# A two-stage attention kernel: energies and group mean placed later, row maxima first on VectorE, and the rounding of the two normalised images traded between ScalarE, VectorE and GpSimd

## The reference, cut to what matters

```python
# x: (8, 32, 32, 256), float32: 8 images of 1024 tokens with 256 channels
def stage0(x):    # local attention: 32 windows of 32 tokens, 8 heads of 32
    q, k, v = split(einsum('bnwc,cd->bnwd', x, w_qkv))
    attn = softmax(einsum('bhnqd,bhnkd->bhnqk', q, k) * 32 ** -0.5)
    out = einsum('bhnqk,bhnkd->bhnqd', attn, v)
    return einsum('bnwc,cd->bnwd', out, w_proj) + b_proj
def stage1(x):    # global attention: one head over all 1024 tokens
    q, k, v = x @ Wq, x @ Wk, x @ Wv        # 32, 32 and 256 channels
    energy = einsum('bid,bjd->bij', k, q)
    return gamma * einsum('bij,bjc->bic', softmax(energy), v)
x = x + stage0(group_norm(x))   # 32 groups of 8 channels, over the whole image
x = x + stage1(group_norm(x))
```

## Time and profile before

| | |
|---|---|
| time, median of 3 runs | 740.21 us (739.8 to 742.75) |
| the profiled execution's own time | 739.61 us |
| its span, first to last instruction | 737.8 us, mean granted clock 0.938 |
| PE busy | 601.7 us (82%) |
| DVE busy | 517.4 us (70%) |
| ACT busy | 298.4 us (40%) |
| POOL busy | 193.5 us (26%) |

### The profile page before, as it was taken

One profiled execution on the slowest core, in us unless ns is written; L12 is line 12 of the kernel. 1 busy time (PEld: TensorE's weight loads), 2 busy tenths in 40 slices (PEclk: granted clock), 3 DMA queues, 4 the chain that ended last, 5 costly groups with the idle time before them and its releaser, 6 DMA issues.

```text
span 737.8 us, 14831 instructions
## 1 busy us (share of the span) xinstructions
PE 601.7 (82%) x5859; PEld 433.7 (59%) x5859; DVE 517.4 (70%) x829; ACT 298.4 (40%) x390; POOL 193.5 (26%) x162
## 2 busy tenths in 40 slices
PE   2565694599798988899898988899888989667987
PEld 2255372457575666657674767666665757444756
DVE  4745367777858878687868877786868785854664
ACT  2323242276125741385225631485226631541071
POOL 4512152303304241305203241305212241002000
PEclk9695896899999999999999999999999999978999
DMA  4032315031421224031502323031502212201001
GB/s 149 15 101 58 85 31 136 2 85 31 122 59 40 67 54 136 16 101 30 145 32 57 71 73 90 14 100 28 151 30 70 61 44 80 69 3 36 29 16 58
DMA packets 40306, 47.51 MB, mean 64 GB/s; under 512 B 6848, under 2 KB 32320, under 8 KB 40256
## 3 DMA queue, kind: packets, MB, share of 16 engines
q1 hardware_dynamic: 36960, 43.47, 22.3%
q10 hardware_dynamic: 3296, 3.34, 1.4%
HBM read 10.09 MB, written 8.39 MB: 25 GB/s over the span
## 4 chain that ended last, share of the span: by engine, by line
PE 54%; DVE 22%; issue 8%; ACT 6%; POOL 5%; SPq 3%; DMA 2%; DVEq 0%; ACTq 0%; POOLq 0%
PE pb L250 7%; PE pb L251 6%; PE pb L252 6%; PE pa L250 6%; PE pa L251 6%; PE pa L252 6%; PE pa L484 4%; PE pb L554 3%; POOL b_nl L1042 3%; DVE a_nh L833 3%; PE pb L536 3%; DVE ast L800 3%; SPq L318 2%; DVE max_neg L896 2%; DVE a_rsum L855 2%
## 5 line engine op out<-in xcount | busy, mean ns | idle before, releaser
L250 PE MATMUL pb<-v_h,e_h 128*128 128x257 f16 x464 | 127.4, 275 | 0.0
L252 PE MATMUL pb<-v_h,e_l 128*128 128x257 f16 x464 | 126.4, 272 | 0.0
L251 PE MATMUL pb<-v_l,e_h 128*128 128x257 f16 x464 | 126.0, 272 | 0.0
L896 DVE TENSOR_REDUCE max_neg<-pb 128x1 f32<-128x1024 f32 x64 | 77.3, 1207 | 65.3 <-PE pb L536 65.3
L911 DVE TENSOR_TENSOR e_l<-e,e_h 128x1024 f16<-128x1024 f32 x64 | 77.8, 1223 | 17.1 <-ACT e L738 15.5
L738 ACT ACTIVATE e<-pb,f_energy 128x1024 f32<-128x1024 f32 x64 | 71.3, 1114 | 14.8 <-PE pb L554 14.8
L1049 POOL TENSOR_TENSOR xb<-xin,bias 128x2048 f32<-128x2048 f32 x8 | 36.3, 4537 | 126.6 <-DVE x L876 126.6
L536 PE MATMUL pb<-q_stack,k_stack 96*128 96x512 f16 x128 | 40.4, 399 | 30.7 <-DMA k_stack<-qk_hl 16.3
L686 ACT ACTIVATE a_xT<-a_xT,anb,ar 128x512 f32<-128x512 f32 x32 | 23.4, 802 | 96.9 <-POOL anb L1033 96.9
L250 PE MATMUL pa<-a_nh,wqkv_h 128*128 128x512 f16 x128 | 50.5, 394 | 11.6 <-DVE before_turn L867 6.0
L1054 POOL TENSOR_TENSOR before_turn<-before_turn,a_rinv 128x1024 f32<-128x1024 f32 x16 | 30.6, 1913 | 89.9 <-DVE a_rinv L857 89.9
(11 more groups left out here) (135 smaller groups left out, 1395.6 us busy)
## 6 DMA issues: line engine op xcount, KB each, us to landing
xin<-in_x SPq DMA_DIRECT2D x16, 512.0 KB, 4.6
diag<-qkT SPq DMA_DIRECT2D x64, 128.0 KB, 2.3
diag<-turned SPq DMA_DIRECT2D x64, 128.0 KB, 2.4
turned<-before_turn SPq DMA_DIRECT2D x128, 64.0 KB, 2.0
out<-y SPq DMA_DIRECT2D x24, 256.0 KB, 2.1
out<-y ACTq DMA_DIRECT2D x8, 256.0 KB, 2.1
q_stack<-qk_hl SPq DMA_DIRECT2D x8, 128.0 KB, 2.3
k_stack<-qk_hl SPq DMA_DIRECT2D x8, 128.0 KB, 2.4
```

The lines of the kernel that those rows point to most:

```text
L250: nc.tensor.matmul(out_ap, lh, rh, start=start, stop=False)
L251: nc.tensor.matmul(out_ap, lh, rl, start=False, stop=False)
L252: return nc.tensor.matmul(out_ap, ll, rh, start=False, stop=stop)
L896: nc.vector.tensor_reduce(max_neg[:, it:it + 1], pb[:, 0:2, :].rearrange("p a n -> p (a n)"), X, ALU.max, negate=True).then_inc(b_max, 1)
```

## The change

Nothing is computed differently. The PE list puts energy 0 and energy 1 each half an output block later, and the group mean and variance of the local image one output block later. The DVE list starts the first half with `a_maximum` and moves row sums and transposes behind row maxima; the group steps of the local image move one maximum later. The rounding of the local image (`a_nh`) goes from DVE to ACT, which computes it straight from the copy with a second activation per piece; `a_out_high` goes ahead of it. The low part of the global image (`b_nl`) goes from POOL to DVE, right behind each rounding.

```diff
@@ PE: group_mean, group_var (the same with u["var"])
-                nc.tensor.matmul(pb[:, 2, u["col"]:u["col"] + CT], group_avg[:], u["mv"][:, :, 0], start=True, stop=True).then_inc(u["s_gm"], 1)
+                nc.tensor.matmul(pb[:, u["mean"], u["col"]:u["col"] + CT], group_avg[:], u["mv"][:, :, 0], start=True, stop=True).then_inc(u["s_gm"], 1)
@@ bufs: a gets mean=3, var=2; b gets mean=2, var=3
@@ PE: first
                     if o and not last_image(i - 1): b_output(i - 1, it, b, range(0, 4))
-                    if b and it == 1: b_energy(i, 0, m)
                     if f and it == 3: transposes("a", i + 2, range(4))
+                    if b and it == 2: b_energy(i, 1, m)
                     if o and not last_image(i - 1): b_output(i - 1, it, b, range(4, 8))
-                    if b and it >= 1: b_energy(i, it, m)
+                    if b and it >= 1: b_energy(i, (0, 2, 3)[it - 1], m)
...
-                    if f and it == 4: group_mean("a", i + 2)
-                    if f and it == 5: group_var("a", i + 2)
+                    if f and it == 5: group_mean("a", i + 2)
+                    if f and it == 6: group_var("a", i + 2)
@@ ACT: normalise
+                if k == "a":
+                    after(act, a_v, nth(b, 4, 0))
                 for c in chunks:
                     for ct in range(CT):
                         v = u["xT"][:, ct, c * CHUNK:(c + 1) * CHUNK]
+                        if k == "a":
+                            nc.scalar.activation(u["nh"][:, ct, c * CHUNK:(c + 1) * CHUNK], v, ACT.Identity,
+                                                 scale=u["r"][:, ct:ct + 1], bias=u["nb"][:, ct:ct + 1]).then_inc(u["s_nh"], 1)
                         nc.scalar.activation(v, v, ACT.Identity,
@@ ACT: first
+                if m: a_out_high(i + 1)
                 if f: normalise("a", i + 2)
-                if m: a_out_high(i + 1)
@@ DVE: norm_high(k, b) becomes b_norm_split(b), called for the global image alone
+                        nc.vector.tensor_copy(b_nh[:, ct, cols], b_xT[:, ct, cols]).then_inc(n_["b"]["nh"], 1)
+                        dve.wait_ge(n_["b"]["nh"], nth(b, 4, j + 1))
+                        nc.vector.tensor_tensor(b_nl[:, ct, cols], b_xT[:, ct, cols], b_nh[:, ct, cols], ALU.subtract).then_inc(n_["b"]["nl"], 1)
@@ DVE: first
-                if m: a_row_sum(i + 1, 0)
                 if m: a_maximum(i + 1, 1)
                 if o: b_result(i - 1, 0)
-                if m: a_transpose(i + 1, 0)
+                if m: a_row_sum(i + 1, 0)
                 if b: b_maximum(i, 0)
-                if m: a_row_sum(i + 1, 1)
                 if o: b_result(i - 1, 1)
                 if b: b_maximum(i, 1)
-                if m: a_transpose(i + 1, 1)
+                if m: a_row_sum(i + 1, 1)
                 if b: b_maximum(i, 2)
+                if m: a_transpose(i + 1, 0)
                 if o: b_result(i - 1, 2)
                 if b: b_maximum(i, 3)
+                if m: a_transpose(i + 1, 1)
                 if o: b_result(i - 1, 3)
                 if f: stats("a", i + 2)
                 if b: b_maximum(i, 4)
-                if f: group_mean("a", i + 2)
                 if o: b_result(i - 1, 4)
                 if b: b_maximum(i, 5)
-                if f: group_scale("a", i + 2)
+                if f: group_mean("a", i + 2)
                 if o: b_result(i - 1, 5)
                 if b: b_maximum(i, 6)
-                if f: norm_high("a", i + 2)
+                if f: group_scale("a", i + 2)
@@ POOL: norm_low(k, b) becomes a_norm_low(b), which waits for s_nh and for s_xn; the call for b goes
```

More of the change, by code:

```diff
@@ L222, in build @@
         )} for k in "ab"}
-        bufs = {"a": dict(src=xin, xT=a_xT, nh=a_nh, nl=a_nl, ps=pa, col=384, **norm["a"], **{"s_" + k: v for k, v in n_["a"].items()}),
-                "b": dict(src=x1, xT=b_xT, nh=b_nh, nl=b_nl, ps=pb, col=0, **norm["b"], **{"s_" + k: v for k, v in n_["b"].items()})}
+        bufs = {"a": dict(src=xin, xT=a_xT, nh=a_nh, nl=a_nl, ps=pa, col=384, mean=3, var=2, **norm["a"], **{"s_" + k: v for k, v in n_["a"].items()}),
+                "b": dict(src=x1, xT=b_xT, nh=b_nh, nl=b_nl, ps=pb, col=0, mean=2, var=3, **norm["b"], **{"s_" + k: v for k, v in n_["b"].items()})}
         def after(eng, s, value):
@@ L401, in group_var @@
                 pe.wait_ge(u["s_var"], nth(b, 1, 1))
-                nc.tensor.matmul(pb[:, 3, u["col"]:u["col"] + CT], group_avg[:], u["e"][:], start=True, stop=True).then_inc(u["s_gv"], 1)
+                nc.tensor.matmul(pb[:, u["var"], u["col"]:u["col"] + CT], group_avg[:], u["e"][:], start=True, stop=True).then_inc(u["s_gv"], 1)
             def project_T(out_ap, wh, wl, cols, c, nh, nl):
@@ L811, in group_mean @@
                 dve.wait_ge(u["s_gm"], nth(b, 1, 1))
-                nc.vector.tensor_scalar(u["gm"][:], pb[:, 2, u["col"]:u["col"] + CT], -1.0, None, ALU.mult).then_inc(u["s_gmc"], 1)
+                nc.vector.tensor_scalar(u["gm"][:], pb[:, u["mean"], u["col"]:u["col"] + CT], -1.0, None, ALU.mult).then_inc(u["s_gmc"], 1)
                 dve.wait_ge(u["s_gmc"], nth(b, 1, 1))
@@ L822, in group_scale, with b_norm_split @@
                 dve.wait_ge(u["s_gv"], nth(b, 1, 1))
-                nc.vector.tensor_scalar(u["ve"][:], pb[:, 3, u["col"]:u["col"] + CT], EPS, None, ALU.add).then_inc(u["s_ve"], 1)
-            def norm_high(k, b):
-                u = bufs[k]
+                nc.vector.tensor_scalar(u["ve"][:], pb[:, u["var"], u["col"]:u["col"] + CT], EPS, None, ALU.add).then_inc(u["s_ve"], 1)
+            def b_norm_split(b):
                 for c in range(CHUNKS):
@@ L829, in norm_high @@
                         j = c * CT + ct
-                        dve.wait_ge(u["s_xn"], nth(b, 4, j + 1))
-                        after(dve, a_v if k == "a" else b_v, nth(b, 4, 0))
-                        nc.vector.tensor_copy(u["nh"][:, ct, c * CHUNK:(c + 1) * CHUNK], u["xT"][:, ct, c * CHUNK:(c + 1) * CHUNK]).then_inc(u["s_nh"], 1)
+                        cols = slice(c * CHUNK, (c + 1) * CHUNK)
+                        dve.wait_ge(n_["b"]["xn"], nth(b, 4, j + 1))
+                        after(dve, b_v, nth(b, 4, 0))
+                        nc.vector.tensor_copy(b_nh[:, ct, cols], b_xT[:, ct, cols]).then_inc(n_["b"]["nh"], 1)
+                        dve.wait_ge(n_["b"]["nh"], nth(b, 4, j + 1))
+                        nc.vector.tensor_tensor(b_nl[:, ct, cols], b_xT[:, ct, cols], b_nh[:, ct, cols], ALU.subtract).then_inc(n_["b"]["nl"], 1)
             def a_copy_k(b, c):
@@ L976, in second @@
                 if m: group_scale("b", i + 1)
-                if m: norm_high("b", i + 1)
+                if m: b_norm_split(i + 1)
                 if f: a_maximum(i + 2, 0)
@@ L1033, in rstd, with a_norm_low @@
                 nc.gpsimd.tensor_tensor(u["nb"][:], u["gm"][:], u["r"][:], ALU.mult).then_inc(u["s_nb"], 1)
-            def norm_low(k, b):
-                u = bufs[k]
+            def a_norm_low(b):
                 for c in range(CHUNKS):
@@ L1040, in norm_low @@
                         cols = slice(c * CHUNK, (c + 1) * CHUNK)
-                        pool.wait_ge(u["s_nh"], nth(b, 4, j + 1))
-                        nc.gpsimd.tensor_tensor(u["nl"][:, ct, cols], u["xT"][:, ct, cols], u["nh"][:, ct, cols], ALU.subtract).then_inc(u["s_nl"], 1)
+                        pool.wait_ge(n_["a"]["nh"], nth(b, 4, j + 1))
+                        pool.nop(nofuse=True)
+                        pool.wait_ge(n_["a"]["xn"], nth(b, 4, j + 1))
+                        pool.nop(nofuse=True)
+                        nc.gpsimd.tensor_tensor(a_nl[:, ct, cols], a_xT[:, ct, cols], a_nh[:, ct, cols], ALU.subtract).then_inc(n_["a"]["nl"], 1)
             def add_bias(b):
@@ L1067, in first @@
                 if f: rstd("a", i + 2)
-                if f: norm_low("a", i + 2)
+                if f: a_norm_low(i + 2)
                 for j in (1, 2):
```

1 line of the change is left out of this document (removed).

## The result

The changed kernel takes 706.91 us (median of 4 runs, 706.33 to 708.19) against 740.0 us (4 runs) of the kernel before on the same chip: a ratio of 0.956, 95% interval 0.954 to 0.958. The forecast was 712 us, 703 to 728. The profiled execution has a span of 706.1 us against 737.8, with a mean granted clock of 0.944 against 0.938.

The account below looks back on a forecast made before the run. PE's list, stretched by DVE's order, was taken as the bound. 22 + 3.0 + 2.5 + 0.5 = 28 us off the execution's 739.61 gave 711.6, median 712 us; 8 in 10 range 703 to 728.

Parts of the forecast that it names:

- The first half of a full step: Energy 0 starts 0.6 us earlier; energies 0 to 6 take 21.6 us plus 0.5 of waits; energy 6 falls 5.3 us earlier.
- ScalarE takes the place of VectorE at the turn: Between the halves of a full step PE waits 2.7 to 3 us for ScalarE; second pass starts 6.1 us earlier.
- The clock: After the wait at the turn PE falls to half clock again, costing 1.6 us in each full step.
- rival 1: The clock does not fall after the turn: 8 us more gained, 704 us; chance 0.14.
- Steps -1 and 0: Before the full steps: step -1 (with -2) 0, earlier `a_out_high` offsetting later low parts; step 0 gains 0.5 us.
- Step 6: Step without a local image, up to its copy of the maxima rows: gains 3.0 us, no clock price or activations.
- rival 2: A late spread or result holds PE mid-step about 2.5 us in each step: 16 us gained, 724 us; chance 0.19.
- rival 3: Slower: energies 0 to 6 come no earlier while mean and variance come later; 746 us; chance 0.05.
- full steps: Steps 1 to 5: 4.4 us gained in each, 22 us together.
- step 7: Gains 2.5 us: 1.3 from half a block, 1.2 from the low part on DVE.
- the rest: Stretch behind step 7's copy of the maxima rows: predicted gain 0.

Follow-up runs that it names:

- experiment 1: Changed kernel with energies 0 and 1 back at their old places in PE's list, half an output block earlier each: 716.2 us, ratio 0.969.
- experiment 2: Changed kernel with VectorE's row sums and transposes back ahead of the row maxima: 720.4 us, ratio 0.973.
- experiment 5: Changed kernel with the local image's group mean and variance back one output block earlier on PE, one maximum earlier on VectorE: 713.0 us, ratio 0.965.
- experiment 6: Changed kernel with the group variance right behind the second half of stage 0's output and epsilon ahead of maximum 6: 691.2 us, ratio 0.934.
- experiment 7: Changed kernel without the second activation per piece of the local image (four instead of eight, result wrong): 685.9 us, ratio 0.926.
- experiment 4: Changed kernel with the local image's rounding back on VectorE behind epsilon, ScalarE with four activations instead of eight: 728.8 us, ratio 0.985.
- experiment 8: Changed kernel with 12 extra unused matmuls in PE's wait at the turn of steps 0 to 5: 700.6 us, ratio 0.947.
- experiment 9: Changed kernel with the local image's rounding back on VectorE only in steps -2, -1 and 0: 715.2 us, ratio 0.967.

## Why the prediction was right, and where a term was off

- **The first half of a full step** held. Energy 0 starts 42.7 to 43.0 us after the second pass (without a fall; before 43.5), so 0.5 to 0.8 us earlier, predicted 0.6. Energies 0 to 6 take 22.73 us, predicted 22.1. From energy 6 to the second pass it is 10.33 us, predicted 10.4 to 10.8. Experiments 1 and 2 show both terms: half a block under the DMA wait, and the order on VectorE. That the later place of the group steps eats its own gain, because epsilon comes later behind the energies, was foretold too; experiments 5 and 6 show it.
- **ScalarE takes the place of VectorE at the turn**: shown by the wait of 3.22 us (predicted 2.7 to 3) and by experiment 7. The extra four activations take 0.70 us each, 2.8 in all, near the 0.73 of the earlier trace rows. Taking the rounding back to VectorE (experiment 4) costs 22 us, though one piece is faster there, 0.43 us against 0.70.
- **The clock** was a fixed price of 1.6 us in each full step in the forecast, and rival 1 was that it does not fall. It is between the two: 1.8 us, in three of the turns of steps 1 to 5. That two of five nearly equal waits were not followed by it was luck: nothing in the prediction says which, or that any would not be. The steps would have come to 77.8 us each with a fall everywhere, against the 77.6 predicted. Experiment 8 shows the price. The prediction leaned on the Trainium skill ("TensorE: Matmul & The Clock Gate", section "HAM oscillation — how this bites in real kernels") for a wait that is paid for in each round. The trace agrees only in part: waits of 5.03 and 5.30 us were paid for in every step, those of 3.2 us in three to five of five, that of 2.87 us in the kernel before in four of five, those up to 1.1 us never.
- **Steps -1 and 0 were mis-sized**: taken as 0 and 0.5 us gained, measured 6.6. The step that failed is the sentence that in step -1 the earlier `a_out_high` gives back what the low parts lose. It priced GpSimd's low parts and left out how late the projection had stood before, behind `a_out_low`, that is behind VectorE's roundings and ScalarE's copies: 3.2 us gained, not 0. In step 0 the 3.3 us of roundings ahead of maximum 7 were named but taken as 0.5; from that projection on, up to the marker, 3.5 us were gained. Experiment 9 gives the roundings' part of both, 6.2 us.
- **Step 6** has gained 0.4 us by its marker, not 3.0: the fall at the turn of step 5 lies behind the marker now, ahead of it before, and counts here. Experiment 8, without it, has 71.9 us for the step, which is 1.5 us gained; half of the 3.0 stays missing. Of that 0.82 us are a wait of TensorE at 582.1 for a result that stands behind the first transpose on VectorE, the kind of wait that rival 2 feared and the forecast had at 0.2 us. **Behind the last marker** 1.6 us are lost by a fall at 676 to 680 us; experiment 1, without one there, has the 37.0 us of before.
- Rivals 2 and 3 did not come in the full steps: no wait over 0.5 us between energies 0 and 7, and the spreads, at 349.98 and 354.09 on SyncE's queue, came in time.

By term: full steps 24.3 us (22 predicted), steps -1 and 0 6.6 (0.5), step 6, step 7 and the rest 0.8 (5.5). In the span that is 31.7 us against 28: the first two errors, 2.3 and 6.1 us too low, outweighed the last, 4.7 too high. That they partly cancelled was luck. The medians are 5 us apart, 706.9 and 712, because the profiled execution of the changed kernel took 708.19 us, 1.3 above its median, where the prediction had put the median 0.6 above the execution.

## What to carry to other kernels

When work moves off an engine, price it in the filling steps of the pipeline too: there the engine has less to do, but more of what it does is waited for. A stall that is moved rather than removed should be followed to the instruction that starts the chain behind it: here epsilon, placed 2.9 us earlier against energy 6, gave nearly as much in the full steps as leaving four activations out. And a wait that is now and then followed by the low clock is worth shortening (behind those of 1.1 us it never fell here) or filling with matmuls.
